# The third token tile of a selective scan is weighted by ScalarE and added to y by GpSimd's accumulating DMA

## The reference

```python
xz = x @ W_in;  xh, z = split(xz)
xc = depthwise_conv3x3(xh)
dt_r, Bp, Cp = split(xc @ W_xproj)
dt = softplus(dt_r @ W_dt + b_dt);  dtN = dt @ W_dtN + b_dtN
# for every token t, in order:
h = exp(dt[:, None] * A) * h + (dtN * B)[None, :] * xc[:, None]     # 512 x 16
y = (h * C[None, :]).sum(states) + Dskip * xc
# after the scan:
y = layernorm(y) * ln_g + ln_b
y = (y * silu(z)) @ W_out + b_out
```

## Time and profile before

| | us |
|---|---|
| median of 3 executions | 5211.84 (5209.93 to 5215.67) |
| the profiled execution: time | 5212.4 |
| the profiled execution: span, first to last instruction | 5210.7 |
| busy: DVE | 4737.3 (91%) |
| busy: PE | 3844.1 (74%) |
| busy: GpSimd | 3264.0 (63%) |
| busy: ScalarE | 2553.0 (49%) |

### The profile page before, as it was taken

The page is one execution under the profiler, slowest core; times in us unless marked ns, Lnnn a source line. Parts: engine busy times, 40 slices in busy tenths (PEclk is TensorE's granted clock), DMA queues, the critical chain, the costliest instruction groups (busy, mean ns, idle before and its releaser), DMA issues.

```text
span 5210.7 us, 71976 instructions
## 1 busy us (share of the span) xinstructions
PE 3844.1 (74%) x20244; PEld 2395.6 (46%) x20244; DVE 4737.3 (91%) x4110; ACT 2553.0 (49%) x3138; POOL 3264.0 (63%) x2570
## 2 busy tenths in 40 slices
PE   4677777777777777777877777777777777777776
PEld 2444445444444444444444444444444444444453
DVE  0999999999999999999999999999999999999994
ACT  1455554445544454445554455545454544554442
POOL 1677666666665666666666566656666666666671
PEclk8888888888888888898888889888888898988877
DMA  2212212221212212221222112211221221112110
GB/s 66 77 50 78 63 44 75 64 70 47 64 60 74 59 44 73 69 62 53 66 61 64 56 56 73 60 56 60 73 66 47 62 75 60 56 58 67 57 37 18
DMA packets 189389, 315.08 MB, mean 60 GB/s; under 512 B 51992, under 2 KB 164120, under 8 KB 188960
## 3 DMA queue, kind: packets, MB, share of 16 engines
q1 hardware_dynamic: 188960, 310.06, 20.0%
HBM read 171.87 MB, written 20.05 MB: 37 GB/s over the span
## 4 chain that ended last, share of the span: by engine, by line
DVE 32%; issue 30%; PE 19%; ACT 8%; POOL 5%; SPq 3%; DVEq 1%; DMA 1%; ACTq 0%; POOLq 0%
DVE st L884 15%; DVE y L867 11%; PE ht L999 5%; POOL st L525 4%; SPq L399 3%; PE work L979 3%; PE work L1084 3%; PE work L1065 2%; ACT decay L655 2%; PE work L1072 2%; ACT L641 1%; PE work L1026 1%; DVE ob L847 1%; ACT xn L751 1%; PE work L1036 1%
## 5 line engine op out<-in xcount | busy, mean ns | idle before, releaser
L525 POOL TENSOR_TENSOR st<-xc,bbc 128x1536 f32<-128x1536 f32 x768 | 2652.8, 3454 | 279.1 <-PE ht L999 176.1
L884 DVE TENSOR_TENSOR_SCAN st<-decay,st 128x1536 f32<-128x1536 f32 x768 | 2568.6, 3345 | 44.4 <-ACT decay L655 21.9
L655 ACT ACTIVATE decay<-dt,neg_a 128x1532 f32<-128x1532 f32 x768 | 1183.2, 1541 | 1994.0 <-DVE st L884 1993.6
L999 PE MATMUL ht<-ident,st 128*128 128x128 f32 x9216 | 1489.2, 315 | 572.4 <-DVE y L867 566.8
L999 PEld LDWEIGHTS ht<-ident,st 128*128 128x128 f32 x9216 | 1230.2, 163 | 897.3 <-DVE y L867 607.6
L867 DVE SCALAR_TENSOR_TENSOR y<-ht,ct,y 128x512 f32<-128x512 f32 x2304 | 1570.3, 736 | 30.0 <-PE ht L999 28.6
L549 POOL COPY carry<-st 128x4 f32<-128x4 f32 x480 | 91.4, 191 | 1130.2 <-DVE st L884 1130.0
L979 PE MATMUL work<-tri,conv_w 96*32 96x384 f32 x4608 | 483.0, 558 | 129.7 <-issue 78.2
L1026 PE MATMUL work<-xn,win 128*128 128x480 f32 x768 | 391.8, 638 | 8.2 <-POOL xn L506 4.4
L1031 PE MATMUL work<-xn,win 128*128 128x384 f32 x768 | 344.7, 603 | 12.6 <-ACT xb L641 11.5
L979 PEld LDWEIGHTS work<-tri,conv_w 96*32 96x32 f32 x4608 | 149.9, 120 | 356.2 <-issue 356.2
(11 more groups left out here) (89 smaller groups left out, 3262.8 us busy)
## 6 DMA issues: line engine op xcount, KB each, us to landing
bbc<-brow SPq DMA_DIRECT2D x192, 768.0 KB, 4.4
tri<-xhp SPq DMA_DIRECT2D x2304, 50.0 KB, 2.0
xin<-in_x_dram SPq DMA_DIRECT2D x48, 384.0 KB, 3.4
out_dram<-ot SPq DMA_DIRECT2D x48, 384.0 KB, 3.4
brow<-bprod SPq DMA_DIRECT2D x48, 24.0 KB, 1.5
win<-in_L_conv_W_in_dram SPq DMA_DIRECT2D x1, 1024.0 KB
wo<-in_L_conv_W_out_dram SPq DMA_DIRECT2D x1, 512.0 KB
w1s<-in_L_conv_W_dram SPq DMA_DIRECT2D x1, 256.0 KB, 3.2
```

Source lines behind the costliest of these rows:

```text
L525: u = g.tensor_tensor(slot, xc[:, kq % 2, :, :], bbc[:, piece_slot(kq, p), n % PIECE, :].unsqueeze(1).to_broadcast([P, DC, T]), ALU.mult)
L655: a.activation(decay[:, :, 1:], dt[:, (k + ahead) % 2, :, 1:], ACT.Exp, scale=neg_a[:, n:n + 1]).then_inc(s_dec, 1)
L884: v.tensor_tensor_scan(state, decay[:, :, :].rearrange("p c t -> p (c t)"), state, 0.0, ALU.mult, ALU.add).then_inc(s_scan, 1)
L999: last = t.transpose(ht[:, m, c * P:(c + 1) * P], st[:, j, c, m * P:(m + 1) * P], ident[:, :])
```

## The change

DVE accumulates only token tiles 0 and 1 (`NTD = 2`). For tile 2, ScalarE multiplies `ht[2]` out of PSUM by the C column into one of two SBUF buffers `weighed` (`weigh`, state s - 1 in step s, ahead of the decay of state s + 1), and GpSimd issues a DMA that adds this buffer to `y[2]` (`accumulate_last`, after `scan_input` and before the layer norm steps and the gates). That DMA waits for ScalarE and for the DMA before it to have landed. PE's transposes into bank 2 wait for ScalarE's `weigh` in place of DVE. The statistics of y tile 2 wait for the last DMA of the pass. To make room, the B rows are multiplied in place in `xp` and not into `bprod`.

```diff
+NTD = NT - 1
-        bprod = sb("bprod", [NS, T])
+        weighed = sb("weighed", [P, 2, D])
+            def accumulate_last(b, k, n, before):
+                kq = (k - before) % K
+                i = (b * K + k - before) * NS + n
+                if n == 0:
+                    await_emptied(pool, b, k, "yi2")
+                need(pool, s_y2, 16 * i)
+                pool.wait_ge(s_wt, i + 1)
+                hold("pool", pool, b)
+                g.dma_start(y[:, kq % 2, NTD, :], weighed[:, n % 2, :], accum_op=ALU.add).then_inc(s_y2, 16)
...
                         scan_input(b, k, 0, 1)
+                    if s >= Y_LAG and "main" in do:
+                        accumulate_last(b, k, s - Y_LAG, 0)
+                    if s < Y_LAG and POST in do:
+                        accumulate_last(b, k, NS - Y_LAG + s, 1)
...
+                def weigh(n, before):
+                    kq = (k - before) % K
+                    i = (b * K + k - before) * NS + n
+                    if n == 0:
+                        await_emptied(act, b, k - 1, "ct")
+                    need(act, s_y2, 16 * (i - 1))
+                    act.wait_ge(s_ht, NT * (i + 1))
+                    a.activation(weighed[:, n % 2, :], ht[:, NTD, :], ACT.Copy,
+                                 scale=ct[:, kq % 2, NTD * NS + n:NTD * NS + n + 1]).then_inc(s_wt, 1)
...
                         normalise_input()
+                    if s >= Y_LAG and main:
+                        weigh(s - Y_LAG, 0)
+                    if s < Y_LAG and post:
+                        weigh(NS - Y_LAG + s, 1)
                     next_decay(s)
...
-                for m in range(NT):
+                for m in range(NTD):
                     dve.wait_ge(s_ht, 3 * i + m + 1)
...
+                            if m < NTD:
+                                dve.wait_ge(s_y, (q0 * NS + NS - 1) * NTD + m + 1)
+                            else:
+                                dve.wait_ge(s_y2, 16 * (q0 + 1) * NS)
                             v.bn_stats(ln_st[:, m, :], y[:, p0, m, :]).then_inc(s_lnst, 1)
...
-                        need(dve, s_brow, q1 * 16)
-                        v.scalar_tensor_tensor(out=bprod[:, :], in0=work[0:NS, jw, 0:T], scalar=bn_rows[:, 0:1],
+                        v.scalar_tensor_tensor(out=xp[0:NS, :], in0=work[0:NS, jw, 0:T], scalar=bn_rows[:, 0:1],
...
-                        need(pe, s_y, NT * i + m - NHT + 1)
+                        if m < NTD:
+                            need(pe, s_y, NTD * (i - 1) + m + 1)
+                        else:
+                            need(pe, s_wt, i)
```

More of the change, by code:

```diff
@@ L271, in vssm_lif_kernel @@
         s_ht = sem("states_transposed")
-        s_y = sem("y_accumulated")
+        s_y = sem("y_accumulated_by_dve")
+        s_wt = sem("last_tile_weighed")
+        s_y2 = sem("last_tile_accumulated")
         s_carry = sem("carry_saved")
@@ L408, in write_rows @@
                 hold("sp", sp, b)
-                sp.dma_start(brow, bprod[:, :]).then_inc(s_brow, 16)
+                sp.dma_start(brow, xp[0:NS, :]).then_inc(s_brow, 16)
                 sp.wait_ge(s_brow, 16 * (q1 + 1))
@@ L694, in evacuate @@
                     elif name == "xp":
-                        await_emptied(act, b, k - 1, "dn")
+                        need(act, s_brow, q1 * 16)
                         bank_copy(name, xp[:, :], T, XP_ROWS)
                     elif name == "ct":
-                        need(act, s_y, (q1 - 1) * NS * NT)
+                        need(act, s_y, (q1 - 1) * NS * NTD)
                         bank_copy(name, ct[:, p1, :].rearrange("p (m n) -> p m n", m=NT), NT * XP_ROWS,
@@ L863, in accumulate @@
                             hold("dve", dve, b)
-                        await_emptied(dve, b, k if m == 2 else k - 1, f"yi{m}")
+                        await_emptied(dve, b, k - 1, f"yi{m}")
                     else:
-                        dve.wait_ge(s_y, 3 * (i - 1) + m + 1)
+                        dve.wait_ge(s_y, NTD * (i - 1) + m + 1)
                     v.scalar_tensor_tensor(out=y[:, kq % 2, m, :], in0=ht[:, m, :],
@@ L897, in iteration @@
                         for m in range(NT):
-                            dve.wait_ge(s_y, (q0 * NS + NS - 1) * 3 + m + 1)
+                            if m < NTD:
+                                dve.wait_ge(s_y, (q0 * NS + NS - 1) * NTD + m + 1)
+                            else:
+                                dve.wait_ge(s_y2, 16 * (q0 + 1) * NS)
                             v.bn_stats(ln_st[:, m, :], y[:, p0, m, :]).then_inc(s_lnst, 1)
```

## The result

The changed kernel takes 5448.45 us (median of 4, 5431.67 to 5461.90) against 5211.74: 1.0452 times the time before, 95% interval 1.0421 to 1.0482, 237 us slower. The forecast was 5250, slower, in a range of 5110 to 5450. The direction is right and the range holds by 1.5 us; the size is wrong: 38 us were forecast, 237 came.

The account below looks back on a forecast made before the run. DVE, 91% busy, was taken as the main bound, with ScalarE's decay chain close under it and other engines holding some steps. Per-pass savings and costs summed to +32 us, with uncounted waking times 5250; range 5110 to 5450.

Parts of the forecast that it names:

- the landing at the turn: Pass end: tile 2's statistics, then scan 1, wait for the last DMA's landing, 2.8 us; 1.4 us more per pass.
- D: Length of GpSimd's one DMA issue per step: between 0.64 and 2.0 us, taken as 1.3.
- Steps 1 to 6: From scan 1 to scan 7 of each pass: 38 us gained over the run, despite 0.5 lost in passes 0 and 5.
- bare steps: Steps with nothing extra: removing 0.65 us from DVE gains only 0.27, since ScalarE's decay chain takes 4.96.
- Step 13: GpSimd's gates, carry and scan input queue behind state 11's DMA; input 14 ready 4.56 + D after scan 13.
- Steps 10 to 12: ScalarE is the bound, its weight op uncovered: scan 10 to 13 takes 19.3 us against 18.09, 1.2 more.
- rival A: The DMA issue is cheap, 0.64 us on GpSimd: about 5107 us, faster; chance 0.30.
- The lock: DVE's two-SBUF-operand ops end with GpSimd's L525: steps 2, 3, 9 gain nothing, except 1.9 us in pass 0's step 9.
- rival C: DVE's saving shows in most steps: 523 us less, 4690; a small part possible, up to 170 less; chance 0.08.
- B: Rival: GpSimd becomes the bound with a DMA issue of 2.0 us, scan 13 to scan 1 30.2: 5466 us; chance 0.12.

Follow-up runs that it names:

- statistics-don't-wait kernel: Changed kernel with tile 2's statistics taken from y tile 1, so DVE doesn't wait for the pass's last DMA; ScalarE waits later: 5234.06 us, ratio 1.0052.
- four-and-last kernel: Against the changed kernel, only states 0, 12, 13, 14 and 15 have tile 2 done by ScalarE and DMA, DVE the others: 5266.84 us, ratio 1.0121.
- weight-op-only kernel: Changed kernel with ScalarE's weight op but without GpSimd's DMA, so tile 2 is never added to y: 5156.42 us, ratio 0.9890.
- DMA-only kernel: Kernel before, DVE doing all three tiles, plus one 256 KB accumulating GpSimd DMA per step between scratch buffers: 5312.65 us, ratio 1.0193.
- two-tile kernel: Changed kernel without token tile 2's accumulation (no weight op, no DMA); PE still transposes all three tiles: 5041.66 us, ratio 0.9682.
- four-state kernel: Against the changed kernel, only states 0, 12, 13 and 14 have tile 2 done by ScalarE and DMA, DVE the other 12: 5133.40 us, ratio 0.9860.

## Why the prediction was right or wrong

**The account.** 5211 - 166 (two tiles on DVE) + 115 (ScalarE's op) + 78 (the DMA on GpSimd, 5156 to 5234) + 214 (DVE's wait for the last landing) = 5452, measured 5448. These are differences from one kernel to the next, so the sum has to come out near the measured time; what it shows is how large each step is, in this order.

**The step that failed** is a term that was sized too small: the landing at the turn, "A transfer of 256 KB lies between 50 KB at 2.0 and 384 KB at 3.4; 2.8." The forecast put this 2.8 behind the end of the DMA's issue, at 16.3 + 5D after scan 13. In the turns out of passes 1 to 3 the trace has, on average:

```
us                             forecast    measured
end of the last DMA's row          22.8        23.4
from there to its landing           2.8         4.5
from the landing to scan 1          1.1         1.1
scan 13 to scan 1                  26.7        29.0
the same before                    25.3        25.2
```

As a typical DMA's landing the 2.8 was right: the median over the run is 3.6 from the row's start, 2.7 from its end. The error was to use a typical value for one particular DMA, which SP's broadcast of 768 KB often meets: 4.2, 5.8 and 6.05 us from its start in the turns shown, 5.2 on average over all passes. The path was right (scan 1 stands behind GpSimd's chain and the landing); it was sized at +1.4 us a pass and measured +3.7. GpSimd's later arrival, 0.6 us, is the smaller part, and nearly all of it is there already at step 12. Removing the wait gives back 214 us in the statistics-don't-wait kernel; the four-and-last kernel loses 133 us by it with five DMAs a pass.

**Steps 1 to 6** are the second term that failed, 112 us worse than forecast. The saving of 0.27 in bare steps is real (scans stand 4.96 to 4.97 apart), and it was lost again in the same stretch. "In passes 0 and 5, where these come late in s = 6, I reckon 0.5 more" is right for these two passes as far as ScalarE goes (0.5 and 0.9 us a pass over before, in the weight-op-only kernel), but ScalarE's op costs in passes 1 to 4 too: in all 62 us in these steps, from two tiles to weight op only. From there the DMAs cost another 68; in the DMA-only kernel they cost 63. The forecast hid D "up to 1.1" there, and took it as 1.3; it put at nothing that a DMA waits for the landing of the one before, 134.8 us of waits over the run, with landings of up to 8.8 us. Some of this stretch hangs on the turn: it is 40 us shorter in the statistics-don't-wait kernel.

**Step 13.** The text named two gates, the carry and the scan input behind the DMA, and left out the memset of the edge rows. PE waits for it in passes 3 and 4 (41.9 us by name), and their step 13 holds 49 of the 56 us. Moving the DMA behind it gave nothing in total.

**Steps 10 to 12**: right in passes 1 to 3. 19.3 forecast, 19.07 measured. Over all passes it is 23 us where 42 were forecast, mainly because pass 4 gained 12 us in place of losing 4.

**D.** 1.3 forecast, 1.35 measured as the period of GpSimd's step less 3.9. The instruction's row has 0.88, which read by itself would have been rival A's case, and A's time of 5107 was far off. The estimate from the Trainium skill ("DMA: Bandwidth & Descriptors", Specifications), 1.07 and about 5200 us, lies further from the measured 1.35 and 5448. The estimate by the form that the Trainium skill gives there for the landing ("Anatomy of one DMA"), 2.6, is 1.0 under the trace's median of 3.6.

**The lock** in pass 0: L893, 3.56 as a median before, was forecast to fall to 1.75 with 1.9 gained in step 9. It did, and step 9 gained 13.7 us over the 8 passes k = 0, 1.7 each. It fell to 1.76 in pass 4 too, which was not forecast: 18.8 us more in step 9 there. In the statistics-don't-wait kernel the same effect, on the op of step 3, gave part of its 214 us (rival C's small part).

**Rivals.** The time is near B's 5466, and B's 30.2 us from scan 13 to scan 1 is near the 29.1 measured over all turns, but B's cause, D = 2.0, is refuted: at 1.35 GpSimd gets there about when forecast, and the landing does the rest. That A is wrong follows from the DMA-only kernel, 105 us slower. C is refuted by the two-tile kernel: with no cost at all for tile 2 it gains 166, not 523.

**Open.** How much of the landing at the turn is due to the broadcast of the B rows was not isolated by a run; that landings with a broadcast near are some 2 us longer is in the timelines, that halving the bytes takes 33 us off step 0 is measured. What lengthens GpSimd's waits in steps 1 to 6 beyond the landings is open as well.

## What to carry to other kernels

An operation moved off the busiest engine has to be followed to the place where its result is read. Here 15 of 16 results were read late and the sixteenth at once, and that one cost most of the loss: with it left on DVE, 159 of 237 us came back. So move only those whose reader is far and whose engine is then the bound: four of 16 states gave a ratio of 0.986, all sixteen 1.045. For a DMA in such a place, take the landing beside the traffic of that moment, not the median over the run. And count a queue's delay from period to period, since the DMA's own row (0.88 us) is only two thirds of what it takes from GpSimd.

## What the runs showed of the hardware that was not expected

GpSimd's operations right behind an accumulating DMA run longer by some 0.3 us: the scan input 3.73 to 3.76 against 3.45, the carry copy 0.49 against 0.19, in the turn of the changed kernel that is shown. Over its whole run the scan input's operation takes 3.74 us as a median where a DMA has started just before it (533 times) and 3.46 where none has (235 times). Ahead of a DMA stand 0.41 to 0.42 us of idle time there even where nothing else is waited for.

The landing of the accumulating DMA over the four-state kernel's run, min/median/max:

```profile
DMA to landing us min/median/max: 3.3/3.8/9.0
```

For 256 KB it is 3.3 us at least and for 128 KB 2.6; carried on to no bytes at all, some 2 us would be left, an estimate from these two sizes. The long ones are in kernels with 192 and with 768 such DMAs alike, up to 9.0 and 8.8 us. In both they go with the broadcast: with a `bbc` copy starting between 1.3 us before and 0.6 us after the DMA the mean is 8.2 us with 192 DMAs and 6.7 with 768, and 3.8 and 3.7 us otherwise.
